# Shared-key attention: lead of two groups, value blocks in halves, and key loads between the send and the put of the maxima

## The reference, cut to what matters

```
def _L2_xattn_ref(q, k, v):              # q: 4 x 512 x 512;  k = v = ctx_512: 4 x 512 x 128
    NUM_Q_HEADS, NUM_KV_HEADS = 32, 8
    ...
    qh = q.reshape(B, S, KV, G, D).transpose(0, 2, 3, 1, 4)    # D = 16, G = 4
    kh = k.reshape(B, S, KV, D).transpose(0, 2, 1, 3)
    vh = v.reshape(B, S, KV, D).transpose(0, 2, 1, 3)
    scores = jnp.einsum('bkgsd,bktd->bkgst', qh, kh) / scale
    weights = jax.nn.softmax(scores, axis=-1)
    out = jnp.einsum('bkgst,bktd->bkgsd', weights, vh)
x = x + _L2_xattn_ref(_layernorm(x, axis=-1), ctx_512, ctx_512)
```

## Time and profile before

| | |
|---|---|
| median of 3 runs | 3659.06 us (3653.41 to 3660.91) |
| the profiled execution's own time | 3620.35 us |
| its span, from first to last instruction | 3618.6 us |
| TensorE, VectorE, ScalarE, GpSimd busy, share of the span | 84%, 62%, 48%, 15% |
| mean granted TensorE clock | 0.919 |
| first shared attention, plain scores of group 0 to the last slot's start | 1589.7 to 1968.7 us |
| second shared attention, the same | 2801.4 to 3182.9 us |

### The profile page before, as it was taken

One profiled execution on the slowest core, in us unless ns is written; L12 is line 12 of the kernel. 1 busy time (PEld: TensorE's weight loads), 2 busy tenths in 40 slices (PEclk: granted clock), 3 DMA queues, 4 the chain that ended last, 5 costly groups with the idle time before them and its releaser, 6 DMA issues. The chain is left out here.

```text
span 3618.6 us, 54338 instructions
## 1 busy us (share of the span) xinstructions
PE 3045.3 (84%) x15486; PEld 2098.8 (58%) x15488; DVE 2256.6 (62%) x3833; ACT 1744.9 (48%) x3082; POOL 545.1 (15%) x1148
## 2 busy tenths in 40 slices
PE   4389997799843999658997798999897899979998
PEld 2167885655622888523332587888785333338886
DVE  5876445588352333479995544666556899845555
ACT  5652223355222555337777433666434577754443
POOL 2320000045403000121111310222121011100000
PEclk8689998899966999859999899999998799989999
DMA  4444445875513333343220442667543322102223
GB/s 141 168 137 148 139 139 175 275 176 147 198 59 129 107 109 104 105 123 97 82 59 20 155 163 95 226 240 243 176 148 101 104 81 62 37 30 95 93 93 116
DMA packets 240799, 460.89 MB, mean 127 GB/s; under 512 B 57413, under 2 KB 73925, under 8 KB 240115
## 3 DMA queue, kind: packets, MB, share of 16 engines
q1 hardware_dynamic: 207314, 342.59, 30.6%
q0 software_dynamic: 22480, 96.23, 7.8%
q10 hardware_dynamic: 10864, 20.45, 1.5%
HBM read 342.73 MB, written 113.77 MB: 126 GB/s over the span
## 5 line engine op out<-in xcount | busy, mean ns | idle before, releaser
L1831 DVE TENSOR_REDUCE at_maxima<-psum 128x1 f32<-128x512 f32 (+1 forms) x768 | 620.4, 859 | 39.1 <-PE psum L1739 33.2
L1812 ACT ACTIVATE at_probs<-psum 128x512 f32<-128x512 f32 x1024 | 528.7, 604 | 206.3 <-PE psum L1755 206.3
L1755 PE MATMUL psum<-at_qT,at_kT 50*128 50x512 f32 x1024 | 372.6, 452 | 75.0 <-ACT at_probs L1812 54.9
L1739 PE MATMUL psum<-at_kT,at_qT 48*128 48x512 f32 x1024 | 387.3, 483 | 12.0 <-DVE at_maxima L1831 9.3
L1755 PEld LDWEIGHTS psum<-at_qT,at_kT 50*128 50x128 f32 x1024 | 169.7, 188 | 365.2 <-ACT at_probs L1812 242.6
L1768 PE MATMUL psum<-at_probs,at_vals 128*32 128x512 f32 x2048 | 277.0, 613 | 0.0
L728 PE MATMUL psum<-ffn_w_hi,ffn_hid_hi 128*128 128x512 f32 x768 | 270.9, 393 | 2.7 <-ACT ffn_hid_hi L776 2.7
L486 PE MATMUL psum<-ident,n_normed 128*128 128x128 f32 x512 | 99.2, 360 | 191.3 <-ACT n_normed L449 128.6
L587 ACT ACTIVATE ffn_w_hi<-ffn_w_raw 128x512 fp32r<-128x512 f32 x262 | 161.5, 633 | 157.6 <-PE psum L733 101.2
L595 DVE TENSOR_TENSOR ffn_w_lo<-ffn_w_raw,ffn_w_hi 128x512 fp32r<-128x512 f32 x262 | 176.4, 685 | 77.5 <-ACT ffn_w_hi L587 77.3
L733 PE MATMUL psum<-ffn_w_hi,ffn_hid_lo 128*128 128x512 f32 x768 | 206.3, 390 | 8.4 <-DVE ffn_hid_lo L834 8.4
(11 more groups left out here) (399 smaller groups left out, 6944.2 us busy)
## 6 DMA issues: line engine op xcount, KB each, us to landing
ffn_w_raw<-in_stream SPq DMA_DIRECT2D x262, 256.0 KB, 2.7
ffn_w_hi<-quantized SPq DMA_DIRECT2D x66, 512.0 KB, 3.5
ffn_w_hi<-quantized SPq DMA_DIRECT2D x65, 256.0 KB, 3.1
at_qT<-q_hi SPq DMA_DIRECT2D x256, 64.0 KB, 2.3
ffn2a_w_raw<-in_shared2a SPq DMA_DIRECT2D x26, 512.0 KB, 3.6
qz_raw<-in_stream SPq DMA_DIRECT2D x16, 768.0 KB, 4.8
quantized<-qz_quant POOLq DMA_DIRECT2D x16, 768.0 KB, 3.8
gathered<-zeros SPq DMA_DIRECT2D x1, 12288.0 KB
```

The source lines that it names most:

```text
L1739: mm = pe.matmul(score[n % 4][:, :], qT[r][half(par, USED), jj, t * P:(t + 1) * P], kT[r][half(par, USED), :], start=True, stop=True)
L1755: pe.matmul(scoreT[turn_of(n)][:, :], kT[r][half(h % 2, USED + 2), t * P:(t + 1) * P], qT[r][half(h % 2, USED + 2), h // 2, :], start=True ...
L1812: act.activation(probs[n % RING][:, :], scoreT[turn_of(n)][:, :], ACT.Exp, scale=factor).then_inc(exped, 1)
L1831: dve.tensor_reduce(maxima[g % 2][:, h:h + banks, t], scores, AX.X, ALU.max).then_inc(maxed, 1)
```

## The change

`LEAD` becomes 2, so `PUT` becomes 1. `RING`, the number of `probs` tiles, becomes 16 instead of 8. Each value block becomes two halves of 256 queries, placed after single pairs by a table. The transposes stand after pair 6 instead of 7. In the SP queue's slot, six of the twelve loads stand between send and put.

```
-    RING, SLOTS, LEAD, AHEAD = 2 * H, 8, 3, 6
+    RING, SLOTS, LEAD, AHEAD = PAIRS, 8, 2, 6
     PUT = LEAD - 1
-    LAST, VALUES, MOVE, RES = 3, (7, 11, 15), 3, 7
+    HALVES = {2: (3, 0, True), 3: (3, 1, True), 8: (0, 0, False), 9: (0, 1, False), 11: (1, 0, False), 12: (1, 1, False), 14: (2, 0, False), 15: (2, 1, False)}
+    MOVE, RES = 3, 6
...
-            def load(g):
+            def load(g, pars=(0, 1)):
...
-                for par in range(2):
+                for par in pars:
...
             for s in range(GROUPS):
                 if s + PUT < GROUPS:
                     send_max(s + PUT)
+                if s + AHEAD < GROUPS:
+                    load(s + AHEAD, (0,))
+                if s + PUT < GROUPS:
                     put_max(s + PUT)
                 if s + AHEAD < GROUPS:
-                    load(s + AHEAD)
+                    load(s + AHEAD, (1,))
...
-            def results(g, t):
+            def results(g, t, part):
+                queries_of = slice(part * S // 2, (part + 1) * S // 2)
...
                 for h in range(H):
                     n = t * H + h
-                    pe.wait_ge(exped, 2 + PAIRS * g + n + 1)
-                    pe.matmul(res[h * OW:(h + 1) * OW, :], vals[g % 2][:, t, :], probs[n % RING][:, :],
-                              start=(t == 0), stop=(t == TB - 1), tile_position=(0, h * OW), skip_group_check=True).then_inc(valued, 1)
+                    if part == 0:
+                        pe.wait_ge(exped, 2 + PAIRS * g + n + 1)
+                    mm = pe.matmul(res[h * OW:(h + 1) * OW, queries_of], vals[g % 2][:, t, :], probs[n % RING][:, queries_of],
+                                   start=(t == 0 and part == 0), stop=(t == TB - 1), tile_position=(0, h * OW), skip_group_check=True)
+                    if part == 1:
+                        mm.then_inc(valued, 1)
...
-                    if n == LAST and s > 0:
-                        results(s - 1, TB - 1)
-                    if n in VALUES:
-                        results(s, VALUES.index(n))
+                    if n in HALVES:
+                        t, part, earlier = HALVES[n]
+                        if not earlier:
+                            results(s, t, part)
+                        elif s > 0:
+                            results(s - 1, t, part)
```

More of the change, by code:

```diff
@@ L1756, in scores_T @@
                           start=True, stop=True).then_inc(scoredT, 1)
-            def results(g, t):
-                if t == 0:
+            def results(g, t, part):
+                queries_of = slice(part * S // 2, (part + 1) * S // 2)
+                if t == 0 and part == 0:
                     pe.wait_ge(vals_kept, g + 1)
@@ L1793, in _ @@
                         turn_results()
-            results(GROUPS - 1, TB - 1)
+            for part in range(2):
+                results(GROUPS - 1, TB - 1, part)
             pe.wait_ge(res_moved, GROUPS)
```

## The result

The change made the kernel slower by 0.8%. The median of six runs is 3674.82 us (3660.6 to 3697.68) against 3652.82 us (3641.05 to 3660.91) of the kernel before in the same comparison. The ratio is 1.0076, interval 1.0048 to 1.0104. That is some 28 us (0.0076 x 3652.8), between 18 and 38. The prediction was 3679 us, +20.2 us, slower with a chance of 0.70.

A forecast was written before the change was run, and what follows sets the result against it. It took a TensorE-ScalarE-TensorE chain to bound the settled slot and the SP queue a stage's start. 7.4 + 7.8 + 0.6 + 3.0 + 1.4 = +20.2 us, on 3659: 3679 us; forecast's own range 3670 to 3688, overall 3645 to 3706.

The forecast's parts named there:

- (a): Main forecast for the whole program: settled slot 11.2 to 11.5 us, total 3670 to 3688 us, chance 0.50.
- The walk: TensorE's settled slot timed, pair by pair and half by half: 11.36 us against 11.22 before.
- The term of 7.8: Slots 2 to 29 of both stages: 56 slots, each 0.14 us slower, +7.8 us.
- (b): Rival on the settled slot: pairs between halves cost 0.33, slot 10.96 us, total 3657 us, chance 0.12.
- (c): Rival on the settled slot: pairs cost 0.33 and the division is in time; 10.76 us, total 3645, chance 0.18.
- Rival (e): Entries into value blocks: each of four added ones costs twice the 0.09, +20 us, total 3699, chance 0.08.
- Rival (d): SP queue: puts land more than 2.0 us later and pace every slot; +28 us, total 3707, chance 0.12.
- The last slots: Last two slots of each stage, where the division isn't late: four slots at 0.15 us, +0.6 us.
- The queue at the start: SP queue at both stages' starts: slot 1 waits about 12 us for the put; +5.0 and +2.4, together 7.4 us.
- The loads between send and put: Six loads queue behind a spill and ahead of the puts: 0.75 us at each of four places, 3.0 us.
- the spill of batch 3: SP queue at slot 10: this spill makes the slot late by 0.7 us a stage, 1.4 us.
- The clock at half behind it: Slot 1, after TensorE's idle stretch at a stage's start: one slot at half clock, taking 13.9 us.

The follow-up runs named there:

- run 9: The kernel before with lead of two groups and six loads between send and put, whole blocks, the change's own queue order: 3629.82 us, ratio 0.9999.
- Run 4: The kernel before with only six of the twelve loads moved between send and put: 3619.44 us, ratio 0.9983.
- run 2: The kernel before with only the lead cut from three groups to two, whole blocks, loads behind the puts: 3641.22 us, ratio 1.0043.
- Run 1: The changed kernel with the lead set back to three groups, halves kept: 3643.42 us, ratio 1.0048 against the kernel before.
- run 3: The changed kernel with loads only four groups ahead and each spill later, behind its slot's puts: 3614.94 us, ratio 0.9975 against the kernel before.
- run 6: The kernel before with lead two, run 3's reordered queue and loads between send and put, whole blocks: 3598.61 us, ratio 0.9938.
- Run 10: run 7's kernel with the last block whole too, so whole blocks behind pairs 2, 8, 11 and 14: 3605.75 us, ratio 0.9926 against the kernel before.
- run 5: The changed kernel again, unedited, for a second profile: 3657.44 us, ratio 1.0100 against the kernel before.
- run 8: run 7's kernel with one extra matmul behind each of the 32 plain scores ahead of slot 0: 3642.19 us, ratio 1.0045 against the kernel before.
- run 7: run 3's kernel with three blocks whole, behind pairs 2, 8 and 11, only the last in halves: 3587.34 us, ratio 0.9898 against the kernel before.

## Why the prediction was right, and where not

**The direction and the size.** +20.2 us was forecast, the comparisons measured 28 (18 to 38) and 36 (25 to 47). That the median, 3674.8, lies below the forecast of 3679 has its cause in the kernel before, which took 3652.8 in the comparison and 3659 in the runs shown first. Slower was right. The slot came as forecast in (a), but the terms of the sum account for only some 12 us of the loss by the first profile and run 9 (6.7 for the queue, 6.7 less 2.1 for the slots, 0.8 for slot 10), as the next paragraphs show; the rest is half clock, for which the sum has one slot a stage. That the time lies so near the forecast is luck in good part.

**The settled slot.** 11.36 forecast, 11.34 measured. The walk held step by step: pair 3 without a wait, 0.43 and 0.57 for a half behind a pair between halves, pair 9 at 5.88. The reciprocal started at 5.03 (forecast 5.02) and pair 9 came 0.85 behind it (forecast 0.86). One step was mis-sized: pair 8 comes behind a stall, and its half stands 0.42 behind it and not 0.33, at 5.24. So pair 9's wait of 0.20 shrinks to about 0.07 (the half ahead of it holds TensorE for 0.64 and not 0.57), too short for the view to show as a wait, and the slot is the same. The term of 7.8 measured 56 x 0.12 = 6.7. That decides rivals (b) and (c): a pair between halves does stand 0.43, and the slot isn't under 11. Rival (e), which the Trainium skill's page "TensorE: Matmul & The Clock Gate", section The mechanism, would give, is out as well: eight blocks entered cost 0.57 + 0.43 each as read, where a load paid whole would have made the slot 0.36 longer. Rival (d) is out: behind slot 1 only slot 10 of the first stage waits for a put, with a DMA share of 0.25 in the settled part.

**The last slots.** I charged 0.15 each for the four without plain scores, +0.6. Slot 30 took 10.57 and not 11.18 in both stages, and slot 31 was shorter too, by some 0.45 (to its last transposes). That makes 2 x (0.61 + 0.45) = -2.1. In the kernel before these slots waited for exponentials just as the others did, so that leaving out the plain scores gave nothing; with the halves TensorE's work sets the pace, and less of it is a gain. The gain isn't steady: in the second profile the half clock came back at the end of both stages, and slot 31 took 16.9 and 18.3 us to its last transposes, where before took 13.3.

**The queue at the start.** The chain was forecast with the spill at 1622.8, puts at 1630.7, slot 1 at 1634.6 and slot 2 at 1648.5. It came as 1624.68, 1632.60, 1636.51 and 1649.74, in a stage that began 1.4 later (1591.1). From the stage's start, slot 2 is at +58.6, forecast +58.8. In the second stage it is at +61.8 against +58.5. Up to slot 4, the loss is 5.1 and 6.0 us beside 8.0 for both by the sum (7.4 and four slots of 0.14). With whole blocks (run 9) it is 4.4 and 2.3, so 6.7 for the 7.4, and the ratio of that kernel is 0.9999, nothing within 7 us. The wait of 12 us takes back the earlier start of slot 0 and the waits of slots 2 and 3 in the old order, and little more.

**The loads between send and put.** I charged 3.0, and 1.4 for the spill of batch 3. Only slot 10 of the first stage waited for its puts, 0.80 us, and in the second stage none did. Run 4 gives -6 us (-13 to +1) for the move alone, and run 9 beside run 2 says the same of it with two groups ahead (0.9999 and 1.0043). What I had wrong there is that I counted the 288 KB ahead of the puts and not the 2.8 us of issue time that move into the queue's idle wait.

**The term that was mis-sized.** "The clock at half behind it" stands in the prediction as one slot of 13.9 us, 2.7 more than a settled one, priced from slot 0. Two things are wrong with that. The price is too low, since slot 0 lacks a value block and the transposes; rows 9, which the prediction used, had it right with 2.46 us for 6.8 at half clock. And the half clock isn't one slot long. At the starts of the second stages it lasted 51.6 and 92.2 us in the two profiles of the change and 78.5 and 81.9 in runs 1 and 3; in their first stages 41.0, 52.3, 41.0 and 27.3. With whole blocks (before, runs 2, 4, 6, 9, 10) it was 27 to 51 us at every start, and with mixed blocks 27 and 31. Slots 1 to 3 of the second stage tell what that costs. In the second profile they took 18.7 + 18.6 + 15.3 = 52.6 us, 18.6 more than three settled ones; in the first profile 16.3 and two settled ones, 5.0 more. That difference of 13.6 is nearly the difference of the two stages (12.8).

**Together.** Run 9 at 0.9999 (0.9981 to 1.0017) and the change at 1.0076 and 1.0100 put the measured loss on the halves, in the change's own order of the queue. (Run 9 also has 8 probs tiles and the transposes after pair 7. Run 10 has the 16 tiles and pair 6 with whole blocks, and has no added half clock: 595 us against 617.) Of it some 7 us are the settled slots, less 2 in the last ones. The rest, some 23 us by the first ratio and 31 by the second with wide intervals, is what the added time at half clock comes to. By the mean granted clock of every execution the changed kernel of run 5 was at half clock for 695 us (median of six) and the kernel before beside it for 608, while run 9 had 613 and before beside it 617. 87 us more at 0.31 to 0.38 for each make 27 to 33 us. Run 1 fits too: 663 against 623 us, so 12 to 15 us, and 3 for the slots, where 17 were measured. That the added half clock lies in the two attentions is shown by the two profiles of the change: 52 us apart in the stages, 50 in the whole program.

On the reordered queue the halves cost less: run 3 had 614 us at half clock and run 6, its like with whole blocks, 586, and the ratios lie 0.37% apart, some 13 us. So the length of the half clock hangs on the blocks and on the queue together. Why is not shown. In the long stretches the profile has TensorE busy throughout, and run 8 lengthened such a stretch with extra matmuls (58 and 55 us at half clock, where run 7 had 31 and 27), but no run tells what ends one, and it varies from execution to execution.

**What beats both.** The halves are worth having once a slot, where they hide the last block's exponential, and not four times; and the shorter lead is worth having once the queue isn't filled with loads and a spill that nobody needs yet. Run 7 does both and is 1.0% faster than the kernel before, 1.8% faster than the change (0.9898 / 1.0076, measured apart).

## What to carry to other kernels

Splitting a block to fill a wait pays only while the wait is longer than the fixed cost of one more entry and exit (0.34 us here), so split the blocks whose wait is the longest and leave the others. Price a stretch at half clock from a slot that does all of the work: the first slot, which lacks a part of it, made it look a third cheaper than it is (0.22 and 0.36). And take a second profile and the mean clock of every execution before you trust the length of such a stretch. And when a lead gets shorter, look at what stands ahead in the queue of the transfer that now comes first; moving loads and a spill behind it was worth more here, together with the shorter lead (0.9938), than the best edit to the engines' work added (from there to 0.9898).

## What the runs showed of the hardware

Granted clock: TensorE busy by the profile 46.30 of 46.30 us and still at 1.2 GHz for all of it (run 8), and slots 1 and 2 of 18.7 and 18.6 us likewise (run 5). I had expected the clock to rise within a slot of steady work. A us at half clock cost 0.29 to 0.44 us in slots behind slot 0 with 4 us of it or more, by the kernel and the slot.

The SP queue has long issues, one of them 1.74 us where the same load otherwise takes 0.42. Some of them stand together with a 16 KB transfer on the queue named "instruction". In the two stages of before such a transfer comes every 21 us, and 23 of the 34 stand within 1 us of an issue of over 0.75 us; in the changed kernel it comes every 15 us, and only 13 of 50 do. Loads behind a spill take 1.2 us as well, with no such transfer near. The page's rows of the DMA queues, first of before:

```profile
q8 instruction: 58, 0.95, 0.1%
```

and of the changed kernel, with 17536 matmuls and transposes on TensorE where before has 15486:

```profile
q8 instruction: 74, 1.21, 0.1%
```

More instructions, more such transfers. That they cause some of the long issues is by their coincidence in time alone; no run tried it.
